# Last stage of a two-part graph network kernel: bias added to x2 by tiles, a third buffer for blocks of counts, product 3 copied out by ScalarE, weight sums placed otherwise

## What is computed

```
def _sage_layer(h, edge_src, edge_dst, deg_inv, W_self, W_neigh, b):
    msg = h[edge_src]
    agg = jax.ops.segment_sum(msg, edge_dst, num_segments=h.shape[0])
    mean = agg * deg_inv[:, None]
    return h @ W_self + mean @ W_neigh + b
...
h = jax.nn.relu(_sage_layer(x, edge_src, edge_dst, deg_inv, W_self0, W_neigh0, b0))
out = _sage_layer(h, edge_src, edge_dst, deg_inv, W_self1, W_neigh1, b1)
...
x = _layernorm(x + _L1_gnn_ref(x, src, dst, ...), axis=-1)
```

## Time and profile before

| what | us |
|---|---|
| median of 3 runs | 1128.74 |
| lowest, highest | 1124.67, 1129.11 |
| the profiled execution, its own time | 1133.16 |
| its span in the trace | 1131.3 |
| TensorE busy | 974.4 (86%) |
| VectorE, ScalarE, GpSimd busy | 745.7, 442.1, 208.4 |
| the last stage's four quarters | from 414 to 1118.8 |

### The profile page before, as it was taken

The page is one execution under the profiler, slowest core; times in us unless marked ns, Lnnn a source line. Parts: engine busy times, 40 slices in busy tenths (PEclk is TensorE's granted clock), DMA queues, the critical chain, the costliest instruction groups (busy, mean ns, idle before and its releaser), DMA issues.

```text
span 1131.3 us, 14312 instructions
## 1 busy us (share of the span) xinstructions
PE 974.4 (86%) x4630; PEld 772.5 (68%) x4630; DVE 745.7 (66%) x1736; ACT 442.1 (39%) x844; POOL 208.4 (18%) x319
## 2 busy tenths in 40 slices
PE   5799898988989989249988989997989989989974
PEld 3476688877888866137766757776767767767753
DVE  7888844647479858149834788722788845787633
ACT  5677642334355773014322234433334312233222
POOL 3000015623533311112000122000132000130000
PEclk9699999999999989769999999999999999999987
DMA  5357673980135844964264343354353463444543
GB/s 191 72 95 204 167 191 113 204 170 0 38 113 174 291 151 156 167 155 135 71 204 151 137 161 112 106 172 117 112 168 114 151 226 127 159 158 127 166 165 124
DMA packets 62163, 164.51 MB, mean 145 GB/s; under 512 B 19379, under 2 KB 20388, under 8 KB 61886
## 3 DMA queue, kind: packets, MB, share of 16 engines
q0 software_dynamic: 18544, 71.90, 23.3%
q1 hardware_dynamic: 33198, 71.64, 21.9%
q10 hardware_dynamic: 10336, 19.85, 5.0%
HBM read 133.09 MB, written 56.02 MB: 167 GB/s over the span
## 4 chain that ended last, share of the span: by engine, by line
PE 52%; DVE 17%; DMA 10%; issue 9%; ACT 7%; POOL 1%; ACTq 0%; DVEq 0%; POOLq 0%
PE bank L2119 18%; PE bank L2103 17%; DMA w_piece<-w_neigh 7%; PE bank L1120 6%; PE bank L1152 4%; PE bank L666 3%; DMA t_dram<-w_piece 2%; DVE h_stage L1869 2%; ACT h_stage L1743 2%; DVE w_piece L1960 2%; PE bank L630 2%; DVE hot_keys L447 1%; ACT squares L1347 1%; DVE hot_src L446 1%; DVE w_slot L1971 1%
## 5 line engine op out<-in xcount | busy, mean ns | idle before, releaser
L2103 PE MATMUL bank<-w_slot,h_stage 128*125 128x512 f32 x1680 | 408.1, 401 | 59.9 <-DVE h_stage L1869 59.2
L2103 PEld LDWEIGHTS bank<-w_slot,h_stage 128*125 128x125 f32 x1680 | 312.4, 188 | 153.5 <-DVE h_stage L1869 77.7
L2119 PE MATMUL bank<-g_rows,a_stage 125*125 125x512 f32 x800 | 200.6, 409 | 31.6 <-issue 31.5
L2119 PEld LDWEIGHTS bank<-g_rows,a_stage 125*125 125x125 f32 x800 | 151.2, 192 | 78.7 <-issue 41.9
L1771 ACT ACTIVATE w_slot<-w_piece 128x512 fp32r<-128x512 f32 x104 | 65.3, 628 | 199.3 <-DVE w_piece L1960 110.1
L2020 DVE SCALAR_TENSOR_TENSOR o<-bank,deg_inv,o 125x512 f32<-125x512 f32 x40 | 30.0, 751 | 131.9 <-PE bank L2119 131.9
L1679 POOL DMA_DIRECT2D w_piece<-w_neigh x80 | 43.4, 554 | 378.6 <-DVE w_slot L1971 205.8
L1152 PE MATMUL bank<-a_turned,gn 125*128 125x418 f32 x360 | 70.9, 354 | 3.9 <-DVE gn L1012 2.9
L1971 DVE TENSOR_TENSOR w_slot<-w_piece,w_slot 128x512 fp32r<-128x512 f32 x104 | 71.0, 683 | 0.0
L1152 PEld LDWEIGHTS bank<-a_turned,gn 125*128 125x128 f32 x360 | 66.9, 188 | 5.7 <-DVE gn L1012 3.5
L1743 ACT ACTIVATE h_stage<-h_turned 128x500 fp32r<-128x500 f32 x60 | 36.9, 624 | 70.7 <-PE bank L2103 52.4
(11 more groups left out here) (236 smaller groups left out, 1341.3 us busy)
## 6 DMA issues: line engine op xcount, KB each, us to landing
a_stage<-at_dram SPq DMA_DIRECT2D x40, 625.0 KB, 6.0
w_piece<-w_neigh POOLq DMA_DIRECT2D x80, 256.0 KB, 3.2
w_piece<-w_self POOLq DMA_DIRECT2D x56, 256.0 KB, 3.0
t_dram<-w_piece ACTq DMA_DIRECT2D x32, 256.0 KB, 2.3
w_piece<-t_dram POOLq DMA_DIRECT2D x32, 256.0 KB, 3.0
at_dram<-a_turned SPq DMA_DIRECT2D x10, 625.0 KB, 9.5
dec_y<-x_bd SPq DMA_DIRECT2D x10, 512.0 KB, 3.8
dec_x<-x_ob SPq DMA_DIRECT2D x10, 512.0 KB, 4.5
```

The lines of the kernel that those rows point to most:

```text
L2103: mm = pe.matmul(bank(q, i)[0:NT, :], st[m % 3][:, a, k, :], slots[w % 3][:, b, k, :], start=(k == 0 and p == 0), stop=(k == HK - 1 and p ...
L2119: mm = pe.matmul(ps_a[u][0:NT, :], cast(a_st[u][0:NT, k, :]), cast(g[0:NT, h, k, :]), start=(n == 0 and h == 0), stop=(n == T - 1 and h == 1))
```

## The change

It has four parts, all in `sage_block` but for one line that hands over more spent semaphores.

1. POOL adds the bias to x2 in ten DMAs of one tile each, ahead of sets 4 to 13 (in quarters 0 and 1), in place of one. SP waits in quarter 2 for all ten.
2. `a_stage` has three buffers; the third lies behind the second, on the place of e as well. Block 1 waits for five and block 2 for nine of the ten low halves of `g_rows`, block t above that for aggregate t - 3.
3. Product 3 is copied from its bank to u by ScalarE (`copy_out`, which replaces `copy_first`). Product 6 is added to e alone, and `join` on VectorE adds e to u later, at jobs 17 to 21. Product 7's eviction waits for its join.
4. Blocks of weights and sums are made at other jobs: the last block of set 3 a job later, set 4 at jobs 13 to 16, set 5 at 20 to 23, set 6 at 24 to 27, set 0 of the next quarter between aggregates instead of at jobs 25 to 28; `third_sum` at jobs 13, 14, 18, 19, 20, `first_sum_again` at 23, 24, 28, 29, 30.

```diff
@@ load_counts, SP
-            u = t % 2
-            if t == 1:
-                sp.wait_ge(g_lo, 10 * q + 5)
-            elif T * q + t >= 2:
-                sp.wait_ge(o_mm, T * q + t - 1)
+            u = t % 3
+            if t in (1, 2):
+                sp.wait_ge(g_lo, 10 * q + (5, 9)[t - 1])
+            elif T * q + t > 0:
+                sp.wait_ge(o_mm, T * q + max(t - 2, 0))
@@ SP, quarter 2
-                sp.wait_ge(x2_biased, 16)
+                sp.wait_ge(x2_biased, 16 * T)
@@ POOL
-            if w == 4:
-                pool.wait_ge(*s.x2_landed[1])
-                pool.dma_start(io["x2_dram"].rearrange("t p d -> (t p) d"), io["sage_b"][1:2, :].to_broadcast([T * 128, D]),
+            if 0 <= w - 4 < T:
+                pool.wait_ge(*s.x2_landed[w % 2])
+                pool.dma_start(io["x2_dram"][w - 4, :, :], io["sage_b"][1:2, :].to_broadcast([128, D]),
                                accum_op=ALU.add).then_inc(x2_biased, 16)
@@ quarter_sets, tile_sets
-        when = ((2, (2, 3, 4, 5)), (3, (6, 8, 10, 11))) if q == 0 else ((3, (5, 7, 9, 11)),)
-        when += ((4, (12, 13, 14, 15)), (5, (16, 17, 18, 19)), (6, (20, 21, 22, 23)), (7, (25, 26, 27, 28)))
+        when = ((2, (2, 3, 4, 5)), (3, (6, 8, 10, 12))) if q == 0 else ((3, (5, 7, 9, 12)),)
+        when += ((4, (13, 14, 15, 16)), (5, (20, 21, 22, 23)), (6, (24, 25, 26, 27)))
...
-        return [(SETS * (q + 1) + n, k) for n, first in ((1, 0), (2, 4)) for k in range(HK) if first + k == t]
+        first = t + sum(t > u for u in (2, 5, 8))
+        return [(SETS * (q + 1) + n // HK, n % HK) for n in range(first, first + (2 if t in (2, 5, 8) else 1)) if n < 3 * HK]
@@ ScalarE
+        def copy_out(q, i):
+            prod, r = JOBS[i]
+            act.wait_ge(p_done, NJ * q + i + 1)
+            if prod == 3:
+                act.wait_ge(g_lo, 10 * q)
+            if prod == 3 and q == 3:
+                act.wait_ge(o_resid, T)
+            act.activation((u2 if prod == 3 else e)[r][0:NT, :], bank(q, i)[0:NT, :], ACT.Copy).then_inc(copied, 1)
...
-            if 1 <= i <= HT:
-                copy_first(q, i - 1)
+            if i > 0 and JOBS[i - 1][0] in (1, 3):
+                copy_out(q, i - 1)
@@ VectorE, evict and join
-            if prod == 3:
...
-                dve.tensor_tensor(u2[r][0:NT, :], mine, e[r][0:NT, :], ALU.add).then_inc(evicted, 1)
             if prod == 6:
-                dve.wait_ge(evicted, evictions(q, PLACE[3, r]))
-                dve.tensor_tensor(e[r][0:NT, :], mine, e[r][0:NT, :], ALU.add)
-                dve.tensor_tensor(u2[r][0:NT, :], mine, u2[r][0:NT, :], ALU.add).then_inc(evicted, 1)
+                dve.wait_ge(copied, copies(q, r))
+                dve.tensor_tensor(e[r][0:NT, :], mine, e[r][0:NT, :], ALU.add).then_inc(evicted, 1)
             if prod == 7:
-                dve.wait_ge(evicted, evictions(q, PLACE[6, r]))
+                dve.wait_ge(joined[0], joined[1] + HT * q + r + 1)
...
+        def join(q, r):
+            dve.wait_ge(copied, copies(q, PLACE[3, r]))
+            dve.wait_ge(evicted, evictions(q, PLACE[6, r]))
+            dve.tensor_tensor(u2[r][0:NT, :], u2[r][0:NT, :], e[r][0:NT, :], ALU.add).then_inc(joined[0], 1)
@@ VectorE, at_job
+            if i in (13, 14, 18, 19, 20):
+                third_sum(q, (13, 14, 18, 19, 20).index(i))
             if 17 <= i < 17 + HT:
-                third_sum(q, i - 17)
-            if 27 <= i < 27 + HT:
-                first_sum_again(q, i - 27)
+                join(q, i - 17)
+            if i in (23, 24, 28, 29, 30):
+                first_sum_again(q, (23, 24, 28, 29, 30).index(i))
```

More of the change, by code:

```diff
@@ L1842, in _ @@
         stage_high(0, 4)
-        copy_first(0, 1)
+        copy_out(0, 1)
         s.fill(act, T - 1)
@@ L1973, in at_job @@
         def at_job(q, i):
-            if i > HT:
+            if i > 0 and JOBS[i - 1][0] not in (1, 3):
                 evict(q, i - 1)
@@ L2092, in job @@
                 before, use = divmod(m - 4, NJ)
-                if use < HT:
-                    pe.wait_ge(e_copied, HT * before + use + 1)
+                if JOBS[use][0] in (1, 3):
+                    pe.wait_ge(copied, copies(before, use))
                 else:
```

29 lines of the change are left out of this document (12 added, 17 removed).

## The result

The changed kernel takes 1082.24 us (median of 4 runs, 1075.68 to 1084.04) beside 1127.08 us for the kernel before in runs on the same chip (1124.67 to 1129.11). The ratio is 0.9592, 95% interval 0.9546 to 0.9639. The forecast was 1059 with a range of 1047 to 1080: the direction was right, the gain was 45 us where about 70 had been forecast, and the time lies 2 us above the range. The profiled execution took 1082.9 us (span 1080.8, granted clock 0.968).

What follows compares the result with a forecast made beforehand. TensorE was taken as the bound, with its idle time and slow clock to be won. Gains of 34 (bias), 10.5 (jobs) and 25.5 (third buffer) sum to 70 us: 1128.7 - 70 = 1059 us, range 1047 to 1080.

Steps and rivals of the forecast that it cites:

- Part 1, the bias: Quarter 0's jobs: ten bias DMAs instead of one remove TensorE's 32.2 us wait and slow clock, gaining 34 us.
- the exposed tile: Bias tiles' delay at sets 3 to 4 of quarters 0 and 1: 1 to 3 us in all, 0 elsewhere.
- A set is needed several jobs later: Jobs of the last stage: at eight of ten tile places the next weight set is needed several 2.81 us jobs later.
- Part 2, VectorE and ScalarE in the jobs: Jobs of quarters 1 to 3: moved work cuts excess time, gaining 2.5, 4 and 4 us, 10.5 in all.
- the circle: Jobs 12 to 21: weight sum, ScalarE's high halves, VectorE's low halves, next sum; 3.23 us per step with one weight block per job.
- the join is one instruction for one taken away: VectorE, jobs 17 to 21: the join replaces one instruction and meets a weight sum only at 20 and 21, already counted.
- Part 3, the third buffer: Aggregates: counts issued 9.5 us ahead instead of 4.7 gain 4.5, 0, 6 and 15 us in quarters 0 to 3, 25.5 in all.
- (a): Aggregates: overlapping transfers share DMA engines, so blocks land later; third buffer gives half, 1072 us, or nothing, 1085; chance 0.12.
- reading of SP's queue: Quarter 1's aggregates: h1's row loads wait for turns ahead of counts, so the third buffer gains 0, staying near 63 us.
- (b): Bias DMAs: ten tiles are as exposed as one piece, 32.2 of 38.9 us, giving 1091 us; chance 0.05.
- (e): Bias tiles: each stops pieces, stores and counts for 11.3 us, 113 in all, giving 1172 us, slower than before; chance 0.02.
- (c): Jobs: the VectorE-ScalarE loop does not shorten because ScalarE's copies lengthen it, giving 1070 us; chance 0.12.

## Why the prediction was too low, step by step

**Part 1, the bias** (34 forecast, 28.6 measured). The mechanism was right: the wait of 32.2 us vanished, ten tiles landed near the foretold 5 to 8 us (median 8.3). The term mis-sized is the exposed tile. It was put at 3 us in all; the first tile alone costs the wait of 4.86 us and 2.9 of slow clock, and without it quarter 0's jobs were 4.5 to 4.8 us shorter. "Five pieces cover 3.9" took the transfer of one tile, while the pieces behind this one landed 10 us after their issues, as the tile did (9.6). Quarter 0 also carries one of the four waits for `w_slot`, 2.6 us. What the forecast did not see at all is that the gain holds only because the same change spreads the sets: with the old places, the kernel is 17 us slower. "A set is needed several jobs later" was true of the new places and was argued as if it were true of any.

**Part 2, VectorE and ScalarE in the jobs** (10.5 in quarters 1 to 3 forecast, -5.2 measured). This step failed, and it is the largest piece of the miss. The forecast's working of the circle was right before (excess 9.3 us computed; in quarter 3 the gaps between low halves exceed a job's 2.81 by 9.6 in all, until they fall below it) and low behind the change (5.0 computed, 6.5 measured in the same quarter). Two costs were not in the sum. First, each set's blocks were compared with the circle, but not with the job that first reads them, a cost put at nothing without a reason: set 5's fourth block, made at job 23, is late for job 25 by 2.6 us in each quarter, 7.7 in these three, with some 1.3 us of slow clock behind it in quarter 3. The row that called for the check was there: VectorE's steps come 3.23 us apart at one block per job, longer than a job of 2.81, so a block made in the last of four such jobs is the latest of them. Second, "the join is one instruction for one taken away" counted instructions, not their place: the join is on the circle, the addition it replaces is not. The forecast's terms for jobs 20 and 21, said to hold the join, are 0.2 and 1.0 us over a job; the gaps there show 1.0 and 0.9 with it and 0.4 and 0.3 with the old evictions. At jobs 17 to 19 it rightly counted nothing, but a set 5 early enough for job 25 makes the joins meet one block more, at job 19. The two kernels that differ in the evictions alone put the price at 5.6 us over quarters 1 to 3. That the old evictions "fill VectorE's wait for ScalarE" was right, and for that reason there was nothing to win by taking them away.

With both costs taken out (set 5 one job earlier, old evictions) the jobs of quarters 1 to 3 were 2.2, 4.2 and 2.3 us shorter than in the earlier trace rows, together 8.7 of the 10.5 forecast, though in that kernel's fastest execution. So the new places do shorten the circle; the late block and the joins hid it.

**Part 3, the third buffer** (25.5 forecast, 30.1 measured). Right in mechanism, low by 4.6 us. Quarter 2 came down to the floor (46.6 us, busy throughout, where 3 us of residual had been left); the DMA share there is 0.80 as rival (a) had computed, with 270 GB/s (257 computed), and no block is late for it. Quarter 3 kept one wait of 3.48 us. For quarter 1 I had said that the third buffer would stand free while SP waits, and that under 60 us would refute it: it took 61.1 (61.2 in the second profile of the kernel before), and with SP's order changed 54.2. The reading of SP's queue holds. What was costed at nothing without naming its cover is the end: stores that had been hidden between slower aggregates now end the kernel, 4.6 us.

**Rivals.** (a) fell, by the aggregates of quarter 2. (b) and (e) fell: one place costs 5 to 8 us, quarter 1's set 4 up to 2, the tiles among quarter 0's aggregates some 2. (c), that the circle doesn't shorten, came nearest to what happened and named half the cause: the new evictions do lengthen the circle, but by the join on VectorE; the copies on ScalarE don't show on it. It gave 1070, since a gain of nought was its floor; the jobs of quarters 1 to 3 became longer than before, which no case on the fast side allowed. With the jobs at -5.2 instead of 10.5 and the end counted, the sum would have been 1059 + 15.7 + 4.6 = 1079.

## What to carry to other kernels

When work is moved to later places, check each piece against its first reader, not only against the throughput of the loop it leaves: a block that is 2.6 us late four times cost 7 us of a change of 45. On a loop between two engines, an instruction's cost depends on its side of the wait; one for one is no trade when one stands in the wait and the other on the path. And parts of one change need each other: the tiles were worth 0.4% alone and 2.3% beside the rest of the change, which only a run with one part undone shows.
